# Attention in one TensorE tiling: 64 rows by 32 columns for scores and values, with two score slots instead of three

## The reference

```python
x = x + 0.5 * ffn(layernorm(x))
x = x + attention(layernorm(x))
x = x + 0.5 * ffn(layernorm(x))

# attention: 16 heads of 16
k, q, v = (einsum('bte,fe->btf', x, W).reshape(B, T, 16, 16) for W in (Wk, Wq, Wv))
k, q = layernorm(k, kln_g, kln_b) * scale, layernorm(q, qln_g, qln_b) * scale
dot = where(causal, -inf, einsum('bihd,bjhd->bhij', q, k))
out = einsum('bhij,bjhd->bihd', softmax(dot), v)
return einsum('bte,fe->btf', out, Wo) + bo

# ffn: base matrix, a shared low-rank pair and the best two of six routed low-rank pairs
return x @ base_W.T + base_b + shared + sum over e of routed[e] * sparse_w[e]
```

## Time and profile before

| | |
|---|---|
| two runs | 1194.8 and 1196.83 us |
| span of the profiled execution | 1192.3 us, first to last instruction |
| TensorE busy | 1104.1 us, 93% |
| ScalarE busy | 1014.7 us, 85%, of it 982.2 in 1056 exponentials |
| VectorE busy | 467.5 us, 39% |
| GpSimd busy | 241.6 us, 20% |

### The profile page before, as it was taken

How to read it: one execution, slowest core, us unless ns; L and a number is a source line. 1 busy time by engine, 2 the same in 40 slices (tenths; PEclk the granted TensorE clock), 3 DMA queues, 4 the chain that set the end, 5 groups by cost and what they waited for, 6 DMA issues and landing times.

```text
span 1192.3 us, 22761 instructions
## 1 busy us (share of the span) xinstructions
PE 1104.1 (93%) x8884; PEld 359.6 (30%) x8884; DVE 467.5 (39%) x1181; ACT 1014.7 (85%) x1134; POOL 241.6 (20%) x377
## 2 busy tenths in 40 slices
PE   3758999999999999999999999999999999999994
PEld 3534333332323233232332232232222222222123
DVE  5678665554544353333333323423131222021114
ACT  3216788789888998999999999999999999999980
POOL 2236533222122211212022021012110101010100
PEclk9779999999999999999999999999999999999996
DMA  5022202003000300003000022000001100000000
GB/s 145 3 63 60 59 11 81 1 28 99 1 1 19 93 17 1 1 32 92 4 1 1 1 67 60 1 1 2 1 10 48 53 1 1 10 10 1 1 19 18
DMA packets 39608, 33.37 MB, mean 28 GB/s; under 512 B 8722, under 2 KB 39432, under 8 KB 39496
## 3 DMA queue, kind: packets, MB, share of 16 engines
q1 hardware_dynamic: 37364, 31.74, 9.0%
q10 hardware_dynamic: 2132, 0.12, 0.1%
HBM read 18.73 MB, written 12.85 MB: 26 GB/s over the span
## 4 chain that ended last, share of the span: by engine, by line
PE 72%; ACT 13%; issue 6%; DVE 6%; DMA 1%; POOL 1%; SPq 0%; ACTq 0%; DVEq 0%; POOLq 0%
PE ps L1190 68%; ACT ring L776 13%; PE ps L1232 2%; PE ps L1298 1%; DMA x<-in_x 1%; DVE st L807 1%; PE ps L1252 1%; DVE area L828 1%; DVE oT L1159 0%; POOL rstd L711 0%; POOL sq L532 0%; DVE x L980 0%; DVE ss L985 0%; DVE sq L1013 0%; ACT area L765 0%
## 5 line engine op out<-in xcount | busy, mean ns | idle before, releaser
L776 ACT ACTIVATE ring<-ps 128x1024 f32<-128x1024 f32 x1056 | 982.2, 1115 | 65.5 <-PE ps L1190 63.5
L1190 PE MATMUL ps<-ring,vf 128*17 128x512 f32 (+3 forms) x4608 | 559.4, 562 | 5.0 <-DVE oT L1159 4.4
L1190 PE MATMUL ps<-queries,keys 50*128 50x512 f16 (+3 forms) x2304 | 363.2, 366 | 22.1 <-ACT ring L776 4.9
L1190 PEld LDWEIGHTS ps<-queries,keys 50*128 50x128 f16 x2304 | 92.3, 93 | 475.3 <-ACT ring L776 437.3
L724 POOL TENSOR_SCALAR_AFFINE_SELECT ring<-ring 128x256 f32<-128x256 f32 (+1 forms) x224 | 103.9, 481 | 396.5 <-ACT ring L776 392.6
L1190 PEld LDWEIGHTS ps<-ring,vf 128*17 128x17 f32 x4608 | 79.7, 95 | 174.5 <-issue 144.2
L711 POOL TENSOR_TENSOR rstd<-var,minus_half 128x4 f32<-128x4 f32 x24 | 24.4, 1017 | 235.6 <-DVE var L813 235.4
L980 DVE SCALAR_TENSOR_TENSOR x<-ps,power,x 128x512 f32<-128x512 f32 x32 | 24.0, 750 | 110.7 <-PE ps L1190 110.7
L846 DVE CAST xnT<-ps 128x512 f16<-128x512 f32 x32 | 22.1, 691 | 100.0 <-PE ps L1232 100.0
L1190 PE MATMUL ps<-baseT,xnT 128*128 128x256 f16 x384 | 55.0, 283 | 3.9 <-DVE area L848 3.8
L1232 PE MATMUL ps<-ident,area 128*128 128x128 f32 x192 | 34.2, 311 | 20.0 <-DVE area L828 20.0
(11 more groups left out here) (153 smaller groups left out, 670.5 us busy)
## 6 DMA issues: line engine op xcount, KB each, us to landing
parts_d<-split SPq DMA_DIRECT2D x32, 256.0 KB, 2.6
keys<-parts_d SPq DMA_DIRECT2D x96, 64.0 KB, 2.3
queries<-parts_d SPq DMA_DIRECT2D x192, 32.0 KB
x<-in_x SPq DMA_DIRECT2D x8, 512.0 KB, 4.2
out_x<-x SPq DMA_DIRECT2D x16, 256.0 KB, 2.2
queries<-shift_d SPq DMA_DIRECT2D x64, 4.0 KB
ring<-in_base_W SPq DMA_DIRECT2D x1, 256.0 KB, 4.9
ring<-in_Wq SPq DMA_DIRECT2D x1, 256.0 KB, 3.8
```

Source lines behind the costliest of these rows:

```text
L776: act.activation(probs[:, u % RING, :], bank(2 * (u % SLOTS), 2), ACTF.Exp, bias=0.0, scale=1.0).then_inc(exp_ok, 1)
L1190: return pe.matmul(o, lhsT, rhs, start=start, stop=stop, skip_group_check=True)
```

## The change

Scores and values get one tiling of 64 rows by 32 columns.

- `scores`: each product of 128 keys becomes four of 32 keys, written to four partition quarters of the same bank; the two heads of a pair, on the two row halves, take turns. Rows and moving columns are as before.
- `values`: each product of 128 keys becomes two of 64, the lower half of the rows into bank `ACC[0]`, the upper half into `ACC[1]`. A batch without a mask is done in two pieces of 256 queries, one after its last unit's own exponential and one a unit later; masked batches stay whole.
- `gather`: VectorE copies the one bank, adds the other, and transposes the sum from the new tile `oS`.
- PSUM: two score slots (banks 0 to 3), two accumulators (4, 5), two side banks in turn (6, 7). Start and end rotate over three and six banks.
- Some small tiles move into `ring` or are shared, to make room for `oS`, and the semaphores for the arrival of keys are two sets in turn.

```diff
-SLOTS = 3
+SLOTS = 2
...
-ACC, SIDE = 6, 7
-START_BANKS = (7, 5, 4, 3)
-END_BANKS = (7, 0, 1, 2, 3, 4, 5)
+ACC, SIDES = (4, 5), (6, 7)
+SIDE = SIDES[1]
+START_BANKS = (7, 6, 3)
+END_BANKS = (6, 7, 0, 1, 2, 3)
+HALF = P // 2
...
         if BATCHES[b][2][-1] == u:
-            values.append((u + (2 if BATCHES[b][3] else 1), b))
+            if BATCHES[b][3]:
+                values.append((u + 2, b, (0, 1)))
+            else:
+                values += [(u + i, b, (i,)) for i in range(2)]
...
-                b = banks[i % len(banks)] if rotate else SIDE
+                b = banks[i % len(banks)] if rotate else SIDES[i % len(SIDES)] if free else SIDE
...
-                    dve.transpose(oT[:, :], bank(ACC)).then_inc(acc_read, 1)
+                    dve.tensor_copy(oS[:, :], bank(ACC[0])).then_inc(*main.own.up())
+                    dve.wait_ge(*main.own.at())
+                    dve.tensor_tensor(oS[:, :], bank(ACC[1]), oS[:, :], ALU.add).then_inc(acc_read, 1)
+                    dve.wait_ge(acc_read, n + 1)
+                    dve.transpose(oT[:, :], oS[:, :]).then_inc(*main.own.up())
...
-                for h, j, q0, w, b, col in blocks:
-                    half = slice(HR * (h % 2), HR * (h % 2) + SH + 2)
-                    m = mm(bank(2 * (u % SLOTS) + b)[:, col:col + w], keys[half, h // 2, j * P:(j + 1) * P],
-                           queries[half, h // 2, q0:q0 + w], True, True)
+                for first, second in zip(blocks[0::2], blocks[1::2]):
+                    for k in range(0, P, 32):
+                        for h, j, q0, w, b, col in (first, second):
+                            half = slice(HR * (h % 2), HR * (h % 2) + SH + 2)
+                            m = mm(bank(2 * (u % SLOTS) + b)[k:k + 32, col:col + w], keys[half, h // 2, j * P + k:j * P + k + 32],
+                                   queries[half, h // 2, q0:q0 + w], True, True)
...
-                blocks = sorted([(q0, h % GH, h, j, w, u, bk, col) for u in units for h, j, q0, w, bk, col in UNITS[u][2]])
-                for q0, k, h, j, w, u, bk, col in blocks:
-                    m = mm(bank(ACC)[32 * k:32 * k + VL, q0:q0 + w], vf[:, j, HEAD[h], :], probs[:, u % RING, bk * CH + col:bk * CH + col + w], first, last)
-                m.then_inc(pv, 1)
+                blocks = [(q0, h % GH, h, j, w, u, bk * CH + col) for u in units for h, j, q0, w, bk, col in UNITS[u][2]]
+                if not masked:
+                    q1 = CH // 2 * parts[0]
+                    blocks = [(q1, k, h, j, CH // 2, u, at + q1) for _, k, h, j, _, u, at in blocks]
+                for q0, k, h, j, w, u, at in sorted(blocks):
+                    for i in range(2):
+                        half = slice(HALF * i, HALF * (i + 1))
+                        m = mm(bank(ACC[i])[32 * k:32 * k + VL, q0:q0 + w], vf[half, j, HEAD[h], :], probs[half, u % RING, at:at + w], first, last)
+                if 1 in parts:
+                    m.then_inc(pv, 1)
```

More of the change, by code:

```diff
@@ L267, in schedule @@
         while values and values[0][0] <= u:
-            b = values.pop(0)[1]
-            yield "values", b
-            if b in GROUP_END:
+            _, b, parts = values.pop(0)
+            yield "values", (b, parts)
+            if b in GROUP_END and 1 in parts:
                 yield "gather", GROUP_END[b]
@@ L273, in schedule @@
         yield from beside(3 * u + 2)
-    for _, b in values:
-        yield "values", b
-        if b in GROUP_END:
+    for _, b, parts in values:
+        yield "values", (b, parts)
+        if b in GROUP_END and 1 in parts:
             yield "gather", GROUP_END[b]
@@ L354, in __init__ @@
         self.parts_out = [s(f"parts_out{b}") for b in range(4)]
-        self.k_in = [[s(f"k_in{c}_{i}") for i in range(2)] for c in range(NC)]
+        self.k_in = [[s(f"k_in{c}_{i}") for i in range(2)] for c in range(2)]
         self.q_in = [s(f"q_in{g}") for g in range(NG)]
@@ L363, in __init__ @@
                 rotate, banks = True, END_BANKS
-                held.update({b: free for b in END_BANKS if b != SIDE})
+                held.update({b: free for b in END_BANKS if b not in SIDES})
             if stage in BANK_STAGES:
                 i = len(self.use)
-                b = banks[i % len(banks)] if rotate else SIDE
+                b = banks[i % len(banks)] if rotate else SIDES[i % len(SIDES)] if free else SIDE
                 parts = stage in SPLIT_STAGES
@@ L459, in build @@
         scaled = sb("scaled", [P, 4])
-        bound = sb("bound", [1, 16])
+        bound = ring[0:1, GEN3 + 24 + 4 * HS:GEN3 + 40 + 4 * HS]
         flag = sb("flag", [1, 1], I32)
@@ L465, in build @@
         var = [sb(f"var{i}", [P, 2, TC]) for i in range(3)]
-        lg, ex, fr, fp, rank = ([sb(f"{q}{f}", [P, TC, NE]) for f in range(2)] for q in ("lg", "ex", "fr", "fp", "rank"))
-        ip = [sb(f"ip{f}", [P, TC, NE], I32) for f in range(2)]
+        lg, ex, rank = ([sb(f"{q}{f}", [P, TC, NE]) for f in range(2)] for q in ("lg", "ex", "rank"))
+        fr, fp, ip = (ring[:, GEN1 + TC * NE * i:GEN1 + TC * NE * (i + 1)].rearrange("p (n e) -> p n e", n=TC) for i in range(3))
         wt = [sb(f"wt{f}", [P, TC, NE + 1]) for f in range(2)]
-        gt, eq = ([sb(f"{q}{f}", [P, TC, NE, NE], BF16) for f in range(2)] for q in ("gt", "eq"))
+        gt, eq = (sb(q, [P, TC, NE, NE], BF16) for q in ("gt", "eq"))
         r3 = [sb(f"r3{f}", [P, 4, TC]) for f in range(2)]
@@ L585, in write_parts @@
                         for i, s in enumerate(PARTS[1]):
-                            sp.dma_start(keys[HR * e + HS * i:HR * e + HS * (i + 1), b % 2 * 4:b % 2 * 4 + 4, t], rows[s, e]).then_inc(K.k_in[c][b % 2], 16)
+                            sp.dma_start(keys[HR * e + HS * i:HR * e + HS * (i + 1), b % 2 * 4:b % 2 * 4 + 4, t], rows[s, e]).then_inc(K.k_in[c % 2][b % 2], 16)
             def fetch(K, c, g):
@@ L1090, in _ @@
             dve.wait_ge(*own.at())
-            dve.tensor_reduce(bound[:, 4:8].unsqueeze(2), gain_rows[:, :, :], AX.X, ALU.add).then_inc(*own.up())
+            dve.tensor_reduce(bound[:, 4:8].unsqueeze(2), gain_rows, AX.X, ALU.add).then_inc(*own.up())
             dve.reciprocal(per, near).then_inc(*own.up())
@@ L1400, in _ @@
                 elif stage == "values":
-                    values(n)
+                    values(*n)
                 elif stage == "projout":
```

67 lines of the change are left out of this document (35 added, 32 removed).

## The result

The changed kernel takes 1289.92 us, the median of two runs (1287.11 and 1292.74), against 1195.82: a ratio of 1.0799, 95% interval 1.0721 to 1.0877. It is slower, as forecast, and by more: 94 us where the forecast had 60.

A forecast was written before the change was run, and what follows sets the result against it. PE led early and was level with ACT late. ACT's idle time would rise from 76 to 133 us: span 1192.3 + 57 + 2.4 = 1251.7, forecast 1256 us with the run median's offset, range 1205 to 1320.

The forecast's parts named there:

- The rhythm: Stretches without side work: PE's work per exponential falls from 0.76 to 0.66 us of 0.92, so ACT stays full.
- The third slot: Two score slots: side work stands between an exponential's end and the next scores; 165 pieces leave ACT idle 118 us.
- The cover of a piece: Time a side work piece may take before ACT idles: 0.26 free on PE plus 0.24 in the loop, 0.50 us.
- The worth of a slot as 0.92 us of cover: Kernel before: third slot counted as 0.92 of the 1.3 us of cover for each side work piece.
- Masked batches: Whole masked values batches: 1.10 us per unit, 0.18 over, lying under the 0.50 of cover; 2 us put down.
- The gather: VectorE's added copy and add before the transpose: mostly hidden, 0 to 8 us, taken as 1; 1.4 more at the end.
- The sum: Whole kernel: ACT idle 133 us instead of 76, +57, plus 2.4, gives span 1251.7; forecast time 1256 us.
- The row halves: Rival, values: row halves served strictly in order make a piece 0.66 us, kernel 1314 us; chance 14%.
- PE can be fed: Rival said it cannot: at 52 ns per weight load and product pair the kernel takes 1600 us; chance 7%.
- The piece is 0.44 and not 0.22: Values piece: forecast took 0.44 us; a rival had 0.22, kernel 1222 us or no change; chance 13%.
- faster: Rival: ACT waits for PE's backlog, not single pieces; with cover about 1.4 us the kernel takes 1161; chance 10%.
- the removed gaps: Tiling changes between scores and values: each of 544 batches loses 2 x 0.10 us on PE, 109 us, all removed.

The follow-up runs named there:

- e1: Kernel before with two score slots instead of three, nothing else changed: 1339.7 us, ratio 1.1211.
- e2: Kernel before with two score slots and unmasked values batches cut in two pieces, old tiling, one accumulator: 1299.6 us, ratio 1.0873.
- e7: Kernel before, three slots kept, with unmasked values batches cut in two pieces, old tiling: 1247.8 us, ratio 1.0453.
- e9: Changed kernel with three slots, values from the lower 64 rows only, one accumulator, one side bank, short gather: 1220.2 us, ratio 1.0189.
- e10: Changed kernel's two slots, but values from the lower 64 rows only, one accumulator, one side bank, short gather: 1382.79 us.
- e4: Changed kernel with unmasked values batches whole, one unit after their last unit: 1315.1 us, ratio 1.1006.
- e6: Kernel before with scores in eight tiles of 64 rows by 32 columns, nothing else changed: 1203.1 us, ratio 1.0078.
- e3: Changed kernel with values of masked batches one unit after their last unit, not two: 1280.53 us, ratio 1.0709.
- e11: Changed kernel with values of masked batches one unit after their last, except each group's first, left at two: 1280.93 us, ratio 1.0714.

## Why the forecast was right, and where its size was off

**The rhythm: right.** Gaps gone, 0.22 from scores to values, a piece of 0.44, 0.92 per exponential in plain stretches, PE with 0.23 free (forecast 0.26).

**The third slot: right, and shown.** The forecast's main step was that each piece of side work now stands in the loop of a slot. Pieces that stand alone show it best, with no mask and no other piece near. The 45 short, 31 middle and 11 long ones delay ACT by 0.23 (median), 1.04 and 1.72 us, where the forecast had 0.19, 0.99 and 1.67. The cover of a piece came out as 0.45, not 0.50: the loop measures 1.61 us, with 0.22 to spare in it, and PE has 0.23. Over 165 pieces 0.05 makes 8 us. The slot by itself is `e1` with 144 us (old tiling, whole batches), `e2` against `e7` with 52 (old tiling, pieces), and `e9` against `e10` with about 79 (new tiling, pieces, half of the values). So its price is no constant: it depends on how evenly PE's work is spread and on what free time PE has.

**The worth of a slot as 0.92 us of cover: not shown.** The forecast gave the kernel before 1.3 us of cover. By the middle and long pieces that stand alone it was 1.1 to 1.2 (0.38 and 0.94 us of delay), and with the new tiling `e9` against `e10` gives 0.4 for the slot. The forecast's sum doesn't use that term.

**Masked batches: the step that failed in size.** The forecast said that they "lie under the 0.50 where nothing else falls in, and I put 2 us on them". The delays for a place in `ring` grew by 36 us. I had counted PE's time for them (1.10 per unit) and not that a whole masked batch is one block of 0.88 us standing behind scores, two units late, with the exponential of u + 5 waiting for its end. This too is the slot's loss and not the tiling's: delays for `ring` are 55 to 57 us in `e1`, `e2`, `e4` and the kernel after, all with two slots, and 21 to 23 in the kernel before, `e6`, `e7` and `e9`, all with three. How much of the 36 is this term alone: `e3` and `e11` take 18 and 16 us back at the full clock. I take it that the rest is late for a second reason as well, a piece of side work or a gather nearby, as it comes back as another wait.

**The gather: small, but perhaps dearer than the 1 us put down.** PE's waits for the accumulator total 4.2 us, against 4.4 before, but the clock was at its lower level for 10 us of the loop against 3. At one group PE waited for the sum, and the clock fell. The kernel after, TensorE and ScalarE:

```profile
607.36 1.22 PE L1202 MATMUL ps<-ring,vf 64*17 64x512 f32 x16 [1.35 <-DVE oS L1169]
...
608.63 1.94 ACT L784 ACTIVATE ring<-ps 128x1024 f32<-128x1024 f32 x2 [2.17 <-PE ps L1202]
...
612.17 1.02 ACT L784 ACTIVATE ring<-ps 128x1024 f32<-128x1024 f32 x1 [1.60 <-PE ps L1202]
```

and windows there (the clock is the third number from the end):

```profile
606.00:608.00 2.00, 0.65 (x17) 0.30 (x24) 1.93 (x3) 0.46 (x1) 1.01 (x3) 1.00 0.04 11
608.00:610.00 2.00, 1.30 (x26) 0.18 (x16) 1.86 (x9) 1.37 (x2) 0.50 (x1) 0.54 0.41 118
610.00:612.00 2.00, 2.00 (x48) 0.86 (x37) 1.90 (x5) 0.57 (x1) 0.53 (x1) 0.50 0.51 119
```

PE worked 0.65 of 2 us, then had a clock of 0.5, and ACT paused 3.8 us.

**The sum: its closeness is in part luck.** Forecast +60, measured +94. The forecast's 118 + 2 + 13 = 133 us are mostly delays, as a piece's cost is reckoned from the pace of 0.92 with the exponential of 1.03 after a pause in the loop. The 76 taken from them are idle time alone. As delays the kernel before has 95, so in one unit the forecast says +38, and the wrong base added 19 of its +57. Against the measured 188.5 us of delays its 133 is short by 55: 13 in what ends with scores (131 for 118, of it 8 the cover), and 42 in the rest (57 for 15), which is the places in `ring`. That scores delays rose by 58 us, close to the forecast's +57, is chance: like for like it had 118 less 73.5, +45. The gather with the clock, 4 us at most, lies inside these delays. Delays that overlap are put to the wait that ended last, so the sizes of the terms are estimates.

**The rivals.** The row halves are not in each other's way: 16 recorded products, two for each fp32 product, end in 0.61 us, not 0.83. They start in two groups of eight, 0.02 us within a group and 0.22 from one to the other. (The Trainium skill, TensorE: Matmul & The Clock Gate, "The mechanism", has matmuls start and end strictly in program order, and I had read that as this rival. The time doesn't bear the rival out; whether the order holds the records don't show, as they don't say which of them are one product.) PE can be fed: 24 pairs of weight load and product go in 0.22 + 0.44 = 0.66 us, 27 ns each. The piece is 0.44 and not 0.22. And "faster" failed with the result itself and with `e1`: of cover near 1.4 us a piece 0.45 is left.

**Why the removed gaps brought nothing.** The trace before had 109 us of gaps on an engine 93% busy. With three slots the pieces cost 54 us in the old tiling and one tiling takes them back (`e7`, then `e9` at the full clock), and the sum is nil. Stretches without side work were at ACT's own pace already. The delays stood at single blocks of side work, which a shorter average does not shorten, and in `e9` the values' earlier place in the order holds PE back as well. How much each of the two weighs was not separated. The Trainium skill (TensorEngine Tiling (Array Packing), "PSUM Bottleneck") says that tiling speeds up TensorE and not the emptying of PSUM; `e9`'s window agrees, PE 5.8 us less busy and the units no faster, though it doesn't tell this cause from the order.

## What to carry to other kernels

Where two engines at 85 and 93% feed each other, count buffers before busy time: a slot gives cover for every block that interrupts. The forecast took it for one period of the slower engine, here 0.92 us. What it gave a middle block was 0.4 us where the order held the other engine back (`e9`, `e10`), and less than 0.1 where that engine had no free time to run ahead (`e7`, `e2`). Work saved on average did not pay for it here. To price it, list the blocks by length and subtract cover, and do this for every wait that the late instruction has, the place it writes to as well as the data it reads. Before counting a removed wait as gain, ask which other one ends just before it; in `e3` 50 of 57 us came back as another. And keep the two sides of a difference in one unit: idle time with idle time, delays with delays.

## What the runs showed of the hardware that I had not expected

- A change of TensorE's tiling cost 0.10 us each way here (values start 0.32 us after the scores before, with 0.22 of stream), and within one tiling next to nothing, though the operands change (0.22 to 0.23 after). Eight tiles of 64 by 32 take 0.41 us for scores where two tiles of 64 by 128 take 0.39.
- With only half of the rows used in the values TensorE's clock fell far more often. `e10` had 1.2 GHz for 334 us and the kernel after, with the same order and the same busy share at the full clock (86.37 of 93.30 us and 86.65 of 93.60), for 10. One such stretch of `e10`:

```profile
300.00:316.00 16.00, 14.19 (x242) 7.11 (x236) 3.97 (x8) 11.22 (x13) 4.14 (x8) 1.00 0.15 51
316.00:364.00 48.00, 46.42 (x528) 20.74 (x528) 12.28 (x28) 29.57 (x30) 7.44 (x11) 0.51 0.21 62
364.00:380.00 16.00, 15.13 (x291) 6.90 (x279) 10.58 (x35) 14.39 (x17) 1.01 (x1) 0.99 0.01 3
```

PE was busy 89% before the fall and 97% during it, where the same work takes longer. With the kernel after at the same share and 10 us, a busy share alone does not tell the clock. Which property of the halved work does it wasn't isolated. It means that leaving half of the work out is no clean way to price a part.
